# One pass for the clustering and the averaging: frequency products between the clustering's steps

## The chip, the cores and the metric

The kernel runs on one core of a Trainium2 chip. A core has TensorE (matmuls, PE in the rows, with its weight loads as PEld), VectorE (DVE), ScalarE (ACT), GpSimd (POOL), and SyncE (SP), which here issues most DMAs. The metric is the time of one execution on the device in microseconds. All data is float32. TensorE's clock can be granted in full (2.4 GHz, shown as 1.00) or at half (1.2 GHz, shown as 0.50).

## The reference, cut to what matters

Two layers over x of 8 batches x 512 channels x 128 x 128. What matters for the change lies in the first:

```python
x = conv(sx, w_down, stride 2, groups)          # 8 x 256 x 64 x 64, "downsampled"
xx = x[0].reshape(256, 4096); xs = (xx - min) / (max - min)
cent = xs[8 picked rows]                         # k-means over the 256 channels
for _ in range(10):
    d = x2 - 2.0 * (xs @ cent.T) + (cent ** 2).sum(1)
    labels = argmin(d); oh = one_hot(labels); cnt = oh.sum(0)
    cent = where(cnt > 0, oh.T @ xs / max(cnt, 1), cent)
labels = argmin(d of the last cent)
v5 = einsum('bchw,ck->bkhw', x, soh / max(scnt, 1))   # mean map of each cluster, all 8 batches
mu, var = gmm_fit(v5)                            # mixture, 10 steps
gate = sigmoid(...)[labels]; out = bilinear_up_x2(w_up * (gate * x + x)) + sx
```

The second layer projects its input, which is that output, on 64 low cosine frequencies, builds linear attention from these 64 numbers per channel, and adds the result. Since upsampling is linear, the kernel gets those 64 numbers from the frequencies of sx and of the downsampled x. So each batch's downsampled x (256 channels x 4096 positions) is needed for two things in the middle of the kernel: its products with 64 frequency columns (q), and its mean over each cluster's channels.

## The kernel before, in words

The program is five passes, with a barrier between them. Each engine has its own instruction stream, written out by hand; semaphores set the order between the engines, and nothing is reordered by a planner.

1. `first_pass` reads x, makes the downsampled x (`xd`, in HBM) on VectorE, and the frequencies of x (`xps`). A turn on TensorE is four transposes of 128 x 128 (L243) and two products with 64 weight columns and 256 moving ones (L255); ScalarE copies the transposed data from PSUM to SBUF between the two (L217). The two products write the two halves of the PSUM partitions, and two small products (L273) add the halves at a batch's end.
2. `cluster_pass` loads batch 0 of `xd`, normalises it on VectorE (L326 to L331), sums its squares on ScalarE (L384), transposes it (L407, copies L388), and makes the 256 x 256 gram matrix with 64 products (L412), since distances to centroids that are means of rows need only products of rows. Then a loop of 11 rounds with three TensorE steps, each of which waits for VectorE and is waited for: gram times weights (L421, four products, result `dot`), the centroids' squares (L426, two products with ones, `c2`), and the counts (L430, two products with ones). VectorE makes the distances, the labels and the new weights from them in some 15 small instructions. SP also loads here what later passes need (`later`, L316).
3. `average_pass` takes the batches one after another, in two pairs of SBUF buffers that SP fills in turn (L476). A batch is 2 x 4096 columns. 16 groups of four 128-column tiles are transposed (L494), copied by ScalarE (L539) and multiplied with q (L505: the data is the stationary side, 128 weight columns, and q moves, 64 columns). Between the last groups stand eight mean chunks of 512 columns (L516), each two products with 128 weight columns: the labels' weights, placed so that a batch fills its own 16 of 128 rows and zeros the others. VectorE adds each chunk to `ft` (L564).
4. `mixture_pass` reads `ft`, runs the mixture, and ends with the gates (`coef`) and the corrected frequencies.
5. `second_pass` is layer 2 and the output: it streams x in and the result out. It uses the frequency table p in SBUF (`all_p`), which stayed there from the first pass on.

In the change's diff, a wait of SP holds back all that SP issues after it: its DMAs are issued in the order of the code.

## Time and profile before

| | us |
|---|---|
| median of 3 runs (3957.73 to 3962.67) | 3962.45 |
| profiled execution | 3954.77 |
| its span, first to last instruction | 3953.1 |
| first DMA of the clustering pass | 1368.07 |
| first DMA of the averaging pass | 1515.89 |
| first DMA of the mixture pass | 1808.36 |
| first DMA of the second pass | 2127.97 |

Over the span TensorE is busy 83%, VectorE 76%, ScalarE 47%, GpSimd 16%. These shares are means over passes with different limits: from 2300 us on, DMA is busy 96% of the time at 338 GB/s, while between 1409 and 1514 us it is idle. The pages' times count from the first instruction.
### The profile page before, as it was taken

To read this page: it belongs to the slowest core of one execution; us is meant where nothing else is said; L and a number is where in the kernel's file an instruction comes from. 1 tells how busy PE (TensorE), PEld (TensorE's weight loads), DVE (VectorE), ACT (ScalarE), POOL (GpSimd) and SP (SyncE) were. 2 spreads that over 40 slices of the span, in tenths; PEclk is the share of its full clock that TensorE was granted. 3 is DMA by queue.
4 is the path that set the end of the run, shared out by engine and by line. 5 is a ranking of instruction groups with operands and counts; after the bars stand their busy time and mean duration, and the time that the engine had idled before them with its cause. 6 is when DMAs were issued, how large, how long until landed. Compare 5 with 4: busy or idle time off the path is not lost. (4 is left out here: it accounts for less than half of the span.)

```text
span 3953.1 us, 68797 instructions
## 1 busy us (share of the span) xinstructions
PE 3294.6 (83%) x23728; PEld 2450.3 (62%) x23728; DVE 3017.8 (76%) x3492; ACT 1872.6 (47%) x4272; POOL 643.5 (16%) x325
## 2 busy tenths in 40 slices
PE   7999999989999467996665788888989887888877
PEld 3454544545545256774444687777878786877876
DVE  5999999999999732114332697988988797978877
ACT  4555555545555211221112355565665555555654
POOL 0000000000000000000000233333333333333333
PEclk9999999999999767997886899999999999999999
DMA  6556465564655303320002499999999999999998
GB/s 279 238 219 271 197 261 228 230 261 199 267 220 238 132 6 139 127 85 0 0 0 76 150 348 326 347 348 337 347 332 336 326 348 322 350 321 345 353 349 310
DMA packets 348926, 945.53 MB, mean 239 GB/s; under 512 B 25938, under 2 KB 58834, under 8 KB 329491
## 3 DMA queue, kind: packets, MB, share of 16 engines
q1 hardware_dynamic: 339346, 907.41, 62.0%
q0 software_dynamic: 9216, 33.56, 2.1%
q8 instruction: 194, 3.18, 0.3%
q14 instruction: 170, 1.38, 0.1%
HBM read 638.89 MB, written 301.99 MB: 238 GB/s over the span
## 5 line engine op out<-in xcount | busy, mean ns | idle before, releaser
L188 DVE SCALAR_TENSOR_TENSOR first_acc<-first_x,first_wd,first_acc 128x1024 f32<-128x1024 f32 (+1 forms) x1088 | 1297.9, 1273 | 57.7 <-ACT first_acc L213 47.1
L1168 PE MATMUL second_o<-second_right,second_left 128*128 128x128 f32 x8192 | 1107.3, 286 | 187.1 <-POOL second_left L960 123.0
L1168 PEld LDWEIGHTS second_o<-second_right,second_left 128*128 128x128 f32 x8192 | 1024.0, 200 | 240.6 <-issue 217.3
L960 POOL TENSOR_TENSOR second_left<-second_mid_copy,second_coef_rep 64x1024 f32<-64x1024 f32 x256 | 608.7, 2378 | 1974.7 <-ACT second_mid_copy L1274 1967.4
L1413 DVE SCALAR_TENSOR_TENSOR second_x<-second_o,second_shift,second_x 128x512 f32<-128x512 f32 x1024 | 734.4, 738 | 236.9 <-PE second_o L1168 233.4
L217 ACT ACTIVATE first_xT<-first_tp 128x512 f32<-128x512 f32 x1024 | 609.2, 598 | 534.6 <-PE first_tp L243 534.1
L243 PE MATMUL first_tp<-all_const,first_x 128*128 128x128 f32 x4096 | 679.4, 291 | 78.7 <-issue 43.6
L243 PEld LDWEIGHTS first_tp<-all_const,first_x 128*128 128x128 f32 x4096 | 442.2, 144 | 460.6 <-issue 447.5
L255 PE MATMUL first_freq<-first_xT,all_p 128*64 128x256 f32 x4096 | 667.3, 407 | 17.0 <-ACT first_xT L217 7.2
L1253 ACT ACTIVATE second_mid<-second_dd,all_inter 128x128 f32<-128x128 f32 x1024 | 327.1, 390 | 381.1 <-DVE second_mid L1395 370.2
L255 PEld LDWEIGHTS first_freq<-first_xT,all_p 128*64 128x64 f32 x4096 | 210.5, 136 | 192.7 <-issue 178.6
L1253 ACT ACTIVATE second_part<-second_dd,all_inter 128x128 f32<-128x128 f32 x1024 | 323.3, 386 | 0.0
L960 DVE TENSOR_TENSOR second_left<-second_mid_t,second_coef_rep 64x1024 f32<-64x1024 f32 x256 | 309.0, 1207 | 7.1 <-PE second_mid_t L1138 5.3
L1138 PE MATMUL second_mid_t<-all_const,second_mid 128*128 128x128 f32 x1024 | 176.1, 299 | 97.8 <-DVE second_mid L1395 97.8
L163 POOL DMA_DIRECT2D downsampled<-first_acc x64 | 34.3, 536 | 1323.8 <-DVE first_acc L188 1127.9
L1274 ACT ACTIVATE second_mid_copy<-second_mid_t 64x512 f32<-64x512 f32 x256 | 151.6, 592 | 169.0 <-PE second_mid_t L1138 141.6
L564 DVE TENSOR_TENSOR gates_ft<-gates_ft,average_mean 128x512 f32<-128x512 f32 x64 | 44.0, 688 | 239.8 <-PE average_mean L516 239.8
L1138 PEld LDWEIGHTS second_mid_t<-all_const,second_mid 128*128 128x128 f32 x1024 | 129.8, 153 | 115.1 <-DVE second_mid L1395 115.1
L1404 DVE TENSOR_TENSOR second_zt<-all_p,second_rr 128x512 f32<-128x512 f32 x128 | 190.4, 1487 | 0.2 <-DVE second_rr L1388 0.2
L1395 DVE TENSOR_TENSOR second_mid<-second_mid,second_part 128x1024 f32<-128x1024 f32 x128 | 154.7, 1209 | 4.3 <-ACT second_part L1253 4.3
L539 ACT ACTIVATE average_dT<-average_tp 128x512 f32<-128x512 f32 x128 | 74.9, 597 | 168.9 <-PE average_tp L494 168.9
L1277 ACT ACTIVATE second_right<-second_zt_t 64x256 f32<-64x256 f32 x256 | 96.7, 378 | 108.1 <-PE second_zt_t L1151 104.9
(216 smaller groups left out, 2468.2 us busy)
## 6 DMA issues: line engine op xcount, KB each, us to landing
second_x<-in_x SPq DMA_DIRECT2D x512, 512.0 KB, 7.6
out<-second_x SPq DMA_DIRECT2D x512, 512.0 KB, 5.7
first_x<-in_x SPq DMA_DIRECT2D x48, 4224.0 KB, 25.2
first_x<-in_x SPq DMA_DIRECT2D x16, 4096.0 KB
second_dd<-downsampled SPq DMA_DIRECT2D x112, 384.0 KB, 6.5
downsampled<-first_acc POOLq DMA_DIRECT2D x64, 512.0 KB, 11.6
average_xd<-downsampled SPq DMA_DIRECT2D x16, 2048.0 KB, 8.3
second_dd<-downsampled SPq DMA_DIRECT2D x16, 320.0 KB, 6.2
```

The source lines that it names most:

```text
L188: nc.vector.scalar_tensor_tensor(out=acc[c][:, :, left:], in0=tap_window(xt[c], (s, dh, dw), OUT1), scalar=wd[:, t, k:k + 1], in1=acc[c][: ...
L217: nc.scalar.activation(xT[slot][:, :, :], tp[slot][:, :, :], ACT.Copy).then_inc(copied[slot], 1)
L243: last = nc.tensor.transpose(tp[slot][:, n * S + s, :], xt[c][:, s, 1 + r + n, :], ident)
L255: last = nc.tensor.matmul(freq_ps[t][n * UV:(n + 1) * UV, 0:S * P], p_sb[:, row, :], xT[slot][:, n * S:(n + 1) * S, :].rearrange("p s g -> ...
L960: return eng.tensor_tensor(left[a][rows, odd:HALF:2, :, :].rearrange("p n (t s) g -> p n t s g", t=T), turned[rows, :, :, :].unsqueeze(3). ...
L1138: last = nc.tensor.transpose(mid_t[:, n, t, :], mid[m % 2][:, t, r:r + 2, :].rearrange("p h w -> p (h w)"), k("ident"))
L1168: last = nc.tensor.matmul(ob[n][:, r, :], left[a][:, r, n, :], right[a][:, r, :], start=True, stop=True)
L1253: last = nc.scalar.activation((mid[c], part)[r][:, :, 2 * i + 1 - e, :], dd[c][:, :, e + r + i, :], ACT.Copy, scale=row_w[:, 2 * e + r, n ...
L1274: nc.scalar.activation(mid_copy[hi, :, :, :], mid_t[hi, :, :, :], ACT.Copy).then_inc(mid_copied, 1)
L1395: nc.vector.tensor_tensor(mid[c][:, :, :, :], mid[c][:, :, :, :], part[:, :, :, :], ALU.add).then_inc(interpolated, 1)
L1404: nc.vector.tensor_tensor(zt[c][:, :, :], p_sb[:, rows, :], rr[:, rows].unsqueeze(2).broadcast_to([P, ROWS2, UV]), ALU.mult).then_inc(zt_m ...
L1413: nc.vector.scalar_tensor_tensor(out=xt[i][:, n // S, n % S, :, :], in0=ob[n][:, :, :], scalar=shift[:, n:n + 1], in1=xt[i][:, n // S, n % ...
```

## The change

`cluster_pass` and `average_pass` become one `gather_pass`.

- TensorE's stream is a row of 128 units, 16 a batch. A unit is four transposes and the two products of the unit before the last, as in the first pass: q is now the stationary side (64 columns), the data moves (256 columns), two units' halves lie in the two halves of PSUM, and a join of two products adds them at the batch's end.
- Between the units of batches 0 to 4 (80 units) stand the clustering's steps: the transposes of the normalised batch at units 10 to 17 and 22 to 29, the gram matrix in eight blocks at 31 to 38, the eleven rounds at 40 to 72, one step a unit, and the labels at 75.
- Squares are summed in eight pieces on ScalarE. The normalised batch goes to a buffer of its own.
- The means come once the labels are known: for batches 4, 5, 6, 7 at the start of units 80, 96, 112 and 128, from the buffers where these batches lie for their frequencies, and then for batches 0 to 3, which are loaded again. A mean is 16 products with 32 weight columns: four chunks of 512 columns in four column quarters of one PSUM bank, the first and second four chunks in the two 16-row parts of a quarter. VectorE copies the bank, and eight DMAs on SP bring its 16-row pieces to their rows of `ft`. A reload stands behind these eight on SP.
- Four buffers of a whole batch take the SBUF space, so p leaves SBUF after the first pass and is loaded again (4 MB) at the start of the second.

The core of the diff (declarations, and steps that only moved, are cut):

```diff
-def cluster_pass(nc, cst, xd, ohn, oh_t, later):
+RING = 4
+EARLY = 5
+UNITS_F = NT // 2
+MEAN_ORDER = [EARLY - 1, *range(EARLY, B), *range(EARLY - 1)]
+RING_OF_FREQ = [b % 2 for b in range(EARLY)] + [1, 2, 3]
+RING_OF_MEAN = [0, 1, 2, 3, 0, 1, 2, 3]
+XX_AT, GRAM_AT, ITER_AT, LABELS_AT = (10, 22), 31, 40, 75
+def gather_pass(nc, cst, q_cols, xd, ohn, oh_t, ft, xpu, later):
...
             @block.sync
+                load(0, 0)
+                sp.dma_start(q_sb[:, :, :], q_cols.rearrange("p (n k) -> p n k", k=UV)).then_inc(const_in, 16)
+                load(1, 1)
                 for dst, src in later:
                     sp.dma_start(dst, src).then_inc(later_in, 16)
+                for b in range(2, B):
+                    i = RING_OF_FREQ[b]
+                    if i < 2:
+                        sp.wait_ge(transposed, (b - 1) * UNITS_F)
+                        if b == 2:
+                            sp.wait_ge(normal, T)
+                    elif i == 2:
+                        sp.wait_ge(x_turned, T * GROUPS)
+                        sp.wait_ge(squared, T * GROUPS)
+                    else:
+                        sp.wait_ge(gram_made, T)
+                    load(i, b)
+                for n, b in enumerate(MEAN_ORDER):
+                    sp.wait_ge(mean_taken, n + 1)
+                    for r in range(POS // 512):
+                        h, j = r // 4, r % 4
+                        at = 32 * j + 2 * K * h
+                        sp.dma_start(flat[b * 2 * K:(b + 1) * 2 * K, r * 512:(r + 1) * 512],
+                                     rows_sb[n % 2][at:at + 2 * K, :]).then_inc(rows_out[n % 2], 16)
+                    if n < EARLY - 1:
+                        load(RING_OF_MEAN[n + B // 2], MEAN_ORDER[n + B // 2])
...
             @block.vector
+                for n in range(B):
+                    dve.wait_ge(mean_made, n + 1)
+                    if n >= 2:
+                        dve.wait_ge(rows_out[n % 2], n // 2 * (POS // 512) * 16)
+                    nc.vector.tensor_copy(rows_sb[n % 2][:, :], mean_ps[n % 2]).then_inc(mean_taken, 1)
...
             @block.scalar
+                for k in range(ends):
+                    x = x_group(k)
+                    if x:
+                        t, n = x
+                        act.wait_ge(x_turned, t * GROUPS + n + 1)
+                        nc.scalar.activation(xsT[:, 4 * n:4 * n + 4, t, :], bank_x[n % 2][:, :, :], ACT.Copy
+                                             ).then_inc(x_copied, 1)
+                        nc.scalar.activation(square[:, :], xx[t][:, n * 512:(n + 1) * 512], ACT.Square,
+                                             accum_out=x2_parts[:, t, n:n + 1]).then_inc(squared, 1)
...
+                    if k < units:
+                        slot = k % SLOTS
+                        act.wait_ge(transposed, k + 1)
+                        nc.scalar.activation(dT[slot][:, :, :], tp[k % 2][:, :, :], ACT.Copy).then_inc(copied[slot], 1)
...
             @block.tensor
+                pe.wait_ge(const_in, 16)
+                def turn(k):
+                    b, u = k // UNITS_F, k % UNITS_F
+                    i = RING_OF_FREQ[b]
+                    if u == 0:
+                        for t in range(T):
+                            pe.wait_ge(d_in[i][t], loads_before(i, b) * 16)
+                    if k >= 2:
+                        pe.wait_ge(copied[(k - 2) % SLOTS], (k - 2) // SLOTS + 1)
+                    for n in range(2):
+                        for t in range(T):
+                            at = (2 * u + n) * P
+                            last = nc.tensor.transpose(tp[k % 2][:, n, t * P:(t + 1) * P], part(i, t)[:, at:at + P],
+                                                       ident)
+                    last.then_inc(transposed, 1)
...
+                    for n in range(2):
+                        last = nc.tensor.matmul(freq_ps[b % 2][n * UV:(n + 1) * UV, 0:T * P], q_sb[:, 2 * u + n, :],
+                                                dT[slot][:, n, :], start=u == 0, stop=u == UNITS_F - 1)
+                    last.then_inc(multiplied[slot], 1)
...
+                def average(n):
+                    b, i = MEAN_ORDER[n], RING_OF_MEAN[n]
...
+                    if n >= B // 2:
+                        for t in range(T):
+                            pe.wait_ge(d_in[i][t], loads_before(i, B + n - B // 2) * 16)
+                    if n >= 2:
+                        pe.wait_ge(mean_taken, n - 1)
+                    for h in range(2):
+                        for t in range(T):
+                            for j in range(4):
+                                r = 4 * h + j
+                                last = nc.tensor.matmul(mean_ps[n % 2][32 * j:32 * j + 32, :],
+                                                        placed[:, t, (1 - h) * 2 * K:(3 - h) * 2 * K],
+                                                        part(i, t)[:, r * 512:(r + 1) * 512],
+                                                        start=h == 0 and t == 0, stop=h == 1 and t == T - 1)
+                    last.then_inc(mean_made, 1)
+                for k in range(ends):
+                    x = x_group(k)
+                    if x:
+                        turn_x(*x)
+                    if GRAM_AT <= k < GRAM_AT + GROUPS:
+                        make_gram(k - GRAM_AT)
+                    if ITER_AT <= k < ITER_AT + 3 * (ITERS + 1):
+                        iterate(k - ITER_AT)
+                    if k == LABELS_AT:
+                        turn_labels()
+                    if k < units:
+                        turn(k)
+                    if 2 <= k < units + 2:
+                        multiply(k - 2)
+                    b, u = k // UNITS_F - 1, k % UNITS_F
+                    if b >= 0 and u == 5:
+                        join(b)
+                    if k >= EARLY * UNITS_F and k % UNITS_F == 0:
+                        average(k // UNITS_F - EARLY)
+                for n in range(B // 2, B):
+                    average(n)
...
@@ second_pass
                     load_rows(0, 0)
                     load_rows(0, 1)
+                    sp.dma_start(p_sb[:, :, :], p_cols.rearrange("w (h k) -> w h k", k=UV)).then_inc(p_in, 16)
...
                     pe.wait_ge(coef_copied, B)
+                    pe.wait_ge(p_in, 16)
                     for u in range(UNITS):
                         stage(0, u, True)
```

How the instructions of TensorE stand in a round of the clustering before (a product here is one row's count, not two records; `dot`, `c` and `cnt` are the three steps):

```order
302 L407 MATMUL cluster_tp<-all_const,cluster_xx 128x128 x64
303 L412 MATMUL cluster_gram<-cluster_xsT 128x256 x64
304 L417 UNCONDITIONAL_BRANCH
305 L417 ISA
306 L421 MATMUL cluster_dot<-cluster_wt,cluster_gram 128x8 x4
307 L426 MATMUL cluster_c<-cluster_prod,all_const 128x8 x2
308 L430 MATMUL cluster_cnt<-cluster_oh,all_const 128x8 x2
```

And now, from unit 40 on (`gather_x` holds the first two steps' results, `gather_count_ps` the counts):

```order
404 L538 MATMUL gather_x<-gather_wt,gather_gram 128x8 x4
405 L570 MATMUL gather_tp<-all_const,gather_d 128x128 x4
406 L580 MATMUL gather_freq<-gather_dT,gather_q 64x256 x2
407 L544 MATMUL gather_x<-gather_prod,all_const 128x8 x2
408 L570 MATMUL gather_tp<-all_const,gather_d 128x128 x4
409 L580 MATMUL gather_freq<-gather_dT,gather_q 64x256 x2
410 L549 MATMUL gather_count_ps<-gather_oh,all_const 128x8 x2
411 L570 MATMUL gather_tp<-all_const,gather_d 128x128 x4
412 L580 MATMUL gather_freq<-gather_dT,gather_q 64x256 x2
```

A unit of frequency work now stands behind each of the three steps, where TensorE had nothing before.

The means on TensorE before, near the end of each batch:

```order
340 L516 MATMUL average_mean<-average_xd_0,average_placed 128x512
341 L516 MATMUL average_mean<-average_xd_1,average_placed 128x512
342 L494 MATMUL average_tp<-all_const,average_xd_1 128x128 x4
343 L505 MATMUL average_freq<-average_q,average_dT 128x64 x4
344 L516 MATMUL average_mean<-average_xd_0,average_placed 128x512
345 L516 MATMUL average_mean<-average_xd_1,average_placed 128x512
```

And now, at the end of the pass:

```order
621 L580 MATMUL gather_freq<-gather_dT,gather_q 64x256 x4
622 L608 MATMUL gather_count_ps<-gather_d,gather_placed 32x512 x16
623 L580 MATMUL gather_freq<-gather_dT,gather_q 64x256 x2
624 L588 MATMUL gather_freq<-all_const,gather_halves 128x64 x2
625 L608 MATMUL gather_gram_ps<-gather_d,gather_placed 32x512 x16
626 L608 MATMUL gather_count_ps<-gather_d,gather_placed 32x512 x16
627 L608 MATMUL gather_gram_ps<-gather_d,gather_placed 32x512 x16
628 L608 MATMUL gather_count_ps<-gather_d,gather_placed 32x512 x16
```

A batch's mean is one block of 16 products with 32 weight columns (the two PSUM banks that held the gram matrix and the counts take turns), and the last five stand with next to nothing between them.

On SP, the end of the pass now reads:

```order
43 L387 DMA gates_ft<-gather_rows1 16x512 x8
44 L359 DMA gather_d3<-downsampled 128x4096 x2
45 L387 DMA gates_ft<-gather_rows0 16x512 x8
46 L387 DMA gates_ft<-gather_rows1 16x512 x8
47 L387 DMA gates_ft<-gather_rows0 16x512 x8
48 L387 DMA gates_ft<-gather_rows1 16x512 x8
```

The reload of the last batch stands behind eight row DMAs of the mean before it, and the row DMAs of the last four means follow; before, SP issued no row DMAs at all.

## Rows read from the trace of the kernel before

**Rows 1.** Timeline: start us, length us, engine, line, instruction; SP and VectorE.

```profile
1368.07 0.82 SPq L313 DMA_DIRECT2D cluster_xx<-downsampled  x2
...
1371.84 0.36 SPq L316 DMA_DIRECT2D all_gam<-in_gamma  x1
...
1808.36 0.31 SPq L624 DMA_DIRECT2D mix_wc<-in_w_conv  x1
...
1810.67 4.42 DVE L720 TENSOR_REDUCE mix_part<-gates_ft 128x64 f32<-128x4096 f32 x1 [3.15 <-DMA mix_wu<-in_w_up]
```

**Rows 2.** Stages: length, PE, PEld, DVE, ACT, POOL busy (instructions), PEclk, DMA share, GB/s.

```profile
400.00:500.00 100.00, 97.01 (x668) 51.89 (x664) 99.07 (x85) 55.29 (x90) 2.66 (x5) 1.00 0.52 210
...
1368.00:1409.50 41.50, 13.80 (x65) 11.04 (x65) 23.27 (x13) 16.46 (x20) 0.00 (x0) 0.56 0.39 144
...
1443.40:1514.00 70.60, 39.26 (x161) 36.41 (x161) 26.66 (x152) 0.00 (x0) 0.00 (x0) 0.50 0.00 0
...
1562.00:1806.00 244.00, 244.00 (x1570) 187.33 (x1569) 41.10 (x63) 67.32 (x119) 0.00 (x0) 1.00 0.26 103
```

**Rows 3.** Timeline of TensorE in the first two clustering rounds; idle before in brackets.

```profile
1438.02 1.05 PE L421 MATMUL cluster_dot<-cluster_wt,cluster_gram 128*128 128x8 f32 x8 [0.66 <-ACT cluster_gram L392]
...
1439.34 0.61 PE L426 MATMUL cluster_c<-cluster_prod,all_const 128*128 128x8 f32 x4 [0.26 <-DVE cluster_prod L344]
...
1441.32 0.61 PE L430 MATMUL cluster_cnt<-cluster_oh,all_const 128*128 128x8 f32 x4 [1.37 <-DVE cluster_oh L359]
...
1443.38 1.88 PE L421 MATMUL cluster_dot<-cluster_wt,cluster_gram 128*128 128x8 f32 x8 [1.45 <-DVEq L373]
...
1445.52 1.02 PE L426 MATMUL cluster_c<-cluster_prod,all_const 128*128 128x8 f32 x4 [0.26 <-DVE cluster_prod L344]
...
1447.92 1.02 PE L430 MATMUL cluster_cnt<-cluster_oh,all_const 128*128 128x8 f32 x4 [1.37 <-DVE cluster_oh L359]
```

**Rows 4.** Timeline of TensorE in the first pass, at its start and around a batch's end.

```profile
25.47 2.82 PE L243 MATMUL first_tp<-all_const,first_x 128*128 128x128 f32 x12 [25.47 <-DMA all_p<-in_p_cols]
...
28.22 1.02 PE L255 MATMUL first_freq<-first_xT,all_p 128*64 128x256 f32 x4
...
29.17 0.66 PE L243 MATMUL first_tp<-all_const,first_x 128*128 128x128 f32 x4
...
589.55 0.66 PE L243 MATMUL first_tp<-all_const,first_x 128*128 128x128 f32 x4
...
590.72 0.65 PE L243 MATMUL first_tp<-all_const,first_x 128*128 128x128 f32 x4
591.52 1.52 PE L255 MATMUL first_freq<-first_xT,all_p 128*64 128x256 f32 x12
593.51 0.66 PE L273 MATMUL first_sum<-all_const,first_halves 128*128 128x64 f32 x4 [0.47 <-ACT first_halves L220]
```

**Rows 5.** Tile cluster_xx: ns min/median/max, first and last start us; DMA landing.

```profile
L384 ACT ACTIVATE cluster_square<-cluster_xx x2: 3617/3617/3617, 1387.7 to 1399.4; 128x4096 f32<-128x4096 f32 x2
L384 ACT ACTIVATION_READ_ACCUMULATOR cluster_square<-cluster_xx x2: 185/186/187, 1391.3 to 1402.9; 128x1 f32 x2
...
DMA to landing us min/median/max: 12.6/12.6/12.6
```

**Rows 6.** Tile cluster_xsT: the gram products and ScalarE's copies.

```profile
L412 PE MATMUL cluster_gram<-cluster_xsT x128: 379/379/483, 1409.5 to 1437.0; 128*128 128x256 f32 x128
L388 ACT ACTIVATE cluster_xsT<-cluster_tp x16: 576/597/599, 1391.3 to 1408.8; 128x512 f32<-128x512 f32 x16
```

**Rows 7.** Timeline of the averaging pass: one mean chunk and what follows it.

```profile
1540.66 1.94 PE L516 MATMUL average_mean<-average_xd,average_placed 128*128 128x512 f32 x4
...
1542.43 0.60 PE L494 MATMUL average_tp<-all_const,average_xd 128*128 128x128 f32 x4
```

**Rows 8.** Stages: ten us near the start of the second pass.

```profile
2136.00:2146.00 10.00, 7.67 (x32) 6.87 (x32) 1.28 (x3) 1.79 (x3) 0.00 (x0) 0.50 1.03 376
```

**Rows 9.** Timeline of the second pass: TensorE's first product that follows the new wait.

```profile
2158.93 5.31 PE L1049 MATMUL second_st<-all_wv,second_xp 128*64 128x512 f32 x8 [6.98 <-DVE second_xp L1354]
```

346 lines of the change are left out of this document (152 added, 194 removed).

## Prediction, written before the changed kernel ran

> **What bounds it now.** I read the views in this order: the whole span by stages with the granted clock, then the stretch between the two passes over x in order of time, then single tiles for what one instruction takes.
>
> The change lies between the first DMA of the clustering pass, at 1368.07 us, and the first DMA of the mixture pass, at 1808.36 us [rows 1]: 440.3 us. All eight batches are averaged after the clustering. In the stages [rows 2] TensorE is busy 39.3 of 70.6 us in the iterations, at clock 0.50, the lower level (1.2 GHz), and 244.0 of 244.0 us at 1.00 (2.4 GHz) in averaging. So the first half of this stretch is bound by a chain of small steps between TensorE and VectorE at a low clock, and the second by TensorE alone.
>
> An iteration took 5.36 us at the high clock (1438.02 to 1443.38) [rows 3]. The later ones go at the lower one: there the four gram products take 1.88 us instead of 1.05, and the two ones-products 1.02 instead of 0.61.
>
> All this is of the profiled execution: span 3953.1, time 3954.8 us. The median of the three runs is 3962.45, 7.7 us above it; I add that at the end.
>
> **The unit of the new loop.** 128 units of four transposes and two frequency products (now 64 weight columns, 256 moving ones) are what the first pass does per turn, with the same shapes. There a turn starts at 589.55 and the next at 590.72: 1.17 us at the high clock [rows 4]. At the low clock twelve transposes took 28.22 - 25.47 = 2.75 us and the two products 29.17 - 28.22 = 0.95, so a unit is 4 x 0.229 + 0.95 = 1.87 us. The low clock lasted 3.7 us after TensorE's start there.
>
> **The sum up to unit 80** (us from 1368.07):
> - Start. TensorE first waits for q, queued behind batch 0. Both halves of batch 0 had landed 12.6 us after issue [rows 5]; q is a quarter of their bytes, so about 2.6 more: 15.2.
> - Units 0 to 9: some 4 us at the low clock are two units, the other eight 9.4: 13.6. The first normalised half was ready at 1387.7, the second at 1399.4 (the squares start there [rows 5]); units 10 and 22 come later than that, so no wait for VectorE.
> - Units 10 to 17 and 22 to 29 also turn a group of the normalised batch. TensorE would need 1.17 + 4 x 0.12 = 1.65. ScalarE does two copies of 512 columns at 0.60 [rows 6], a square of 512 (an eighth of 3.62 would be 0.45; I take a copy's 0.60) and an accumulator read of 0.19 [rows 5]: 1.99, and it is what ends last. 16 x 1.99 = 31.8. Bounds 1.65 and 2.2 each (waits between): 26 to 35.
> - Five plain units (18 to 21, 30): 5.9.
> - Gram, eight blocks of eight products. 128 records start over 27.5 us, 0.217 each [rows 6]; eight products are 16 records, 3.5, and a unit 1.17: 8 x 4.66 = 37.3. Unit 39: 1.2. TensorE does this work as before, and nothing hides it.
> - Iterations, 11 x 3 units. The gram products take 1.05, then a unit 1.17: 2.22, more than the 1.32 that VectorE needs until the next step. From the c2 products to the counts took 1.98 and from the counts to the next gram products 2.06 [rows 3]; there 0.61 + 1.17 = 1.78 fit in. So 2.22 + 1.98 + 2.06 = 6.26, and 68.9 for eleven. This is the heart of the gain: the 33 units (38.6 us) cost almost nothing, and TensorE idles 0.5 of 6.26 us.
> - Units 73 to 79 and two turned labels: 8.7. Four joins (a batch's two halves added, four records, 0.66 as in the first pass's fold [rows 4]): 2.6.
>
> Together 15.2 + 13.6 + 31.8 + 5.9 + 37.3 + 1.2 + 68.9 + 8.7 + 2.6 = 185.2.
>
> **From unit 80 on.** 48 units and three joins: 56.2 + 2.0, to 243.4. To this the means. Before, a chunk's two products (four records of 512 columns) took 1542.43 - 1540.66 = 1.77 us [rows 7], eight chunks 14.2 a batch. Now there are again 16 products a batch, as many columns each, but with 32 weight columns in one quarter of the array. No row shows quarters. Bounds: one after another, 14.2; four at a time, 3.5. The nearest row is the run of twelve records on two halves: 1.52 us from first start to last end [rows 4], where one at a time needs 12 x 0.217 = 2.6. Halves gave the full two, so I take the full four: 3.5.
>
> The Trainium skill ("TensorE: Matmul & The Clock Gate", Part 3: Packing small matmuls) says that matmuls start strictly in program order. Since a product is two records on one quarter, neighbours alone could overlap then, two at a time: 7.1 a batch, a rival below. The trace speaks against it: in strict order the twelfth record would start six steps of 0.217 after the first and end 0.38 later (a record's drawn length [rows 6]), 1.68 and not 1.52. By the same part's 2.38 times for three column tiles, a batch would be an estimated 4.5 us, and the sum some 6 us higher.
>
> Means 0 to 3 stand in the loop: 4 x 3.5, to 257.4. After that, the last batch's products and join take 1.9 and means 4 to 6 10.5, but mean 7 needs batch 3 loaded again into the buffer that mean 3 frees: VectorE's copy 0.9 (ScalarE's takes 0.60, and a wake-up), eight row DMAs queued on SP ahead of the load at 0.54 each (seven issues from 1368.07 to 1371.84 [rows 1]) 4.3, landing 12.6, together 17.8. That is later than 12.4, so the load decides: 275.2, mean 7 to 278.7. Then the tail that the old pass had not: copy 0.9, eight issues 4.3, landing 2.3 (as 1808.36 to 1810.67 [rows 1]), end of the pass 0.8: 287.0. The other reloads have 18 us or more of units to hide in. The 64 additions of VectorE go away, but they lay beside a TensorE that was busy all the time.
>
> **Outside the stretch.** The first pass is unchanged. The second pass loads p again, 4.2 MB, behind the first rows of downsampled data and ahead of x. DMA moved 376 GB/s between 2136 and 2146 [rows 8], so p is 11.2 us of it, and lands before 2150. TensorE and VectorE wait for it ahead of work that began at 2158.93 [rows 9]. x comes 11 us later than it did, before any sum needs it. I cost it at 0; if the cover went, 11.2.
>
> **Total.** 440.3 - 287.0 = 153.3 saved. 3954.8 - 153.3 = 3801.5, plus 7.7: **3809 us**.
>
> **Rivals.**
> 1. *Quarters only in pairs.* 7.1 a batch: 243.4 + 28.4 + 1.9 + 21.3 + 7.1 + 8.3 = 310.4, the reload now hidden. Saved 129.9: 3833. For it: nothing in the trace runs more than two at once. Against: the full overlap of halves.
> 2. *Quarters don't run in parallel at all,* so that this part of the change doesn't do what it says: 243.4 + 56.8 + 1.9 + 56.8 + 8.3 = 367.2, saved 73.1: 3889. Against: halves do.
> 3. *The iterations stay at the low clock.* A low-clock iteration needs 1.88 + 1.87, and twice 1.02 + 1.87: 9.5 us instead of 6.26. 11 x 3.3 = 36: 3845. For it: clock 0.50 through the old iterations with TensorE busy 56% of the time. Against: it is now busy 92%, with units that held 1.00 in the first pass [rows 2].
> 4. *Slower: the low clock holds in the whole new pass.* Units 128 x 1.87 = 239.4, turned groups 14.7, gram 55.8, iterations' own products 11 x 3.92 = 43.1, joins 9.1 + 2.9, means in pairs at half speed 113.6, labels 0.6, start and tail 23.5: 502.7, 62.4 more than now: 4025. With four quarters at once it is 445.9, or 3968. It becomes slower once more than 129.9 / 192.3 = 68% of the pass is at the low clock. For it: the clock is 0.50 when the pass starts, and 0.56 on average until the gram products [rows 2]. Against: the old averaging pass, a mix of the same kinds, held 1.00 for 244 us.
>
> On rival 4, the skill (same page, Part 4: PE-mode transpose) says that transposes do not hold the high clock as matmuls do, and here transposes are half of a unit. By that rule alone rival 4 would be likely. The trace does not agree: the first pass, made of the same units, has 1.00 over 100 us [rows 2].
>
> **Chances.** Forecast 57%, pairs 25%, not parallel 5%, iterations at the low clock 8%, whole pass low 2%, other 3%. The forecast's terms move by -9 (group turns at 1.65, smaller tail) and +15 (waits in the iterations, slower landing), so 3800 to 3824. The range takes in pairs and most of the low iterations: 3790 to 3855. It leaves out about a fifth. A measurement of this kernel tells 0.2%, 8 us, from no change: faster 97% (all but rival 4 and a part of "other"), within 1%, slower 2%.
>
> **What would show it.** Units 1.17 us apart at clock 1.00; iterations 6.3 us apart; a mean's 16 products in 3.5 us (7.1 for pairs); a gap of about 5 us ahead of the last mean, filled by the reload; first mixture DMA 287 us after the first load; second pass as long as now. Wrong would be: a clock of 0.50 past unit 10, ScalarE late in plain units, or TensorE held by a reload of batches 0 to 2.

## The result, and the profile of the changed kernel

The changed kernel takes 3865.89 us (median of 4 runs, 3862.28 to 3875.95), the kernel before 3960.09 in the same comparison. The ratio is 0.976, 95% interval 0.973 to 0.980. The forecast was 3809 us, with a range from 3790 to 3855: the sign was right, the size not. 94 us were gained where 153 had been worked out. Between the two profiled executions, 3954.8 and 3866.2 us, the gain is 88.6, 65 less than worked out.

The profiled execution has a span of 3864.6 us. It shows where the 65 us are (the first loads are issued at 1368.07 and 1368.89 us):

| stretch | before | forecast | measured |
|---|---|---|---|
| first load to first mixture DMA | 440.3 | 287.0 | 318.1 |
| of that, first load to the first mean | | 185.2 | 209.3 |
| of that, first mean to the end | | 101.8 | 108.8 |
| first mixture DMA to the labels' last products | 311.2 | unchanged | 344.4 |
| from there to the end | 1833.5 | unchanged | 1833.2 |

The fourth row of the table ends at these products, in the kernel before and in the changed one (ns min/median/max, first and last start us):

```profile
L688 PE MATMUL mix_l<-mix_ymat,gates_oh_t x4: 361/361/380, 2119.6 to 2120.3; 128*128 128x8 f32 x4
```

```profile
L757 PE MATMUL mix_l<-mix_ymat,gates_oh_t x4: 361/362/383, 2031.4 to 2032.0; 128*128 128x8 f32 x4
```

So the forecast failed in two places: 31 us in the new pass, and 33 us in the mixture pass, whose code was not touched.

Stages of the changed kernel, to be held against [rows 2]. Columns: stretch, length, busy time of PE, PEld, DVE, ACT and POOL, granted clock, DMA share, GB/s.

```profile
1368.90:1467.50 98.60, 83.24 (x512) 57.82 (x512) 23.64 (x15) 40.95 (x92) 0.00 (x0) 0.90 0.51 200
1467.50:1480.00 12.50, 11.15 (x85) 7.51 (x83) 5.26 (x30) 3.91 (x8) 0.00 (x0) 1.00 0.00 1
1481.00:1569.70 88.70, 88.70 (x367) 58.58 (x366) 24.08 (x139) 17.60 (x32) 0.00 (x0) 0.50 0.46 190
1569.70:1655.00 85.30, 84.66 (x626) 40.81 (x628) 2.96 (x5) 34.69 (x64) 0.00 (x0) 1.00 0.43 160
1655.00:1721.00 66.00, 23.48 (x136) 10.84 (x128) 29.11 (x51) 6.39 (x11) 0.00 (x0) 0.63 0.27 81
1721.00:2038.00 317.00, 219.66 (x934) 134.25 (x934) 92.64 (x252) 42.41 (x68) 0.00 (x0) 0.72 0.00 0
```

Row 1 is the way to the clustering rounds, row 2 the first two rounds, row 3 most of the others. There TensorE is busy for the whole 88.7 us, and yet at 0.50. A busy share of 100% does not say that the clock is up. Row 4 is the units with the means, row 5 the end of the pass, row 6 the mixture's rounds.

TensorE in the first round, and in a later one, by the timeline (start us, us, engine, line, instruction, and in brackets the idle time before):

```profile
1467.54 1.06 PE L538 MATMUL gather_x<-gather_wt,gather_gram 128*128 128x8 f32 x8
...
1469.60 0.61 PE L544 MATMUL gather_x<-gather_prod,all_const 128*128 128x8 f32 x4
...
1471.58 0.61 PE L549 MATMUL gather_count_ps<-gather_oh,all_const 128*128 128x8 f32 x4 [0.30 <-DVE gather_oh L436]
...
1473.65 1.06 PE L538 MATMUL gather_x<-gather_wt,gather_gram 128*128 128x8 f32 x8 [0.38 <-DVEq L450]
```

```profile
1495.27 1.02 PE L549 MATMUL gather_count_ps<-gather_oh,all_const 128*128 128x8 f32 x4
1496.14 1.09 PE L570 MATMUL gather_tp<-all_const,gather_d 128*128 128x128 f32 x4
1497.17 1.12 PE L580 MATMUL gather_freq<-gather_dT,gather_q 128*64 128x256 f32 x4
1498.22 1.88 PE L538 MATMUL gather_x<-gather_wt,gather_gram 128*128 128x8 f32 x8
```

The first round takes 1473.65 - 1467.54 = 6.11 us, with 0.68 us of waiting in it, where 6.26 was forecast. At the low clock a unit takes 1498.22 - 1496.14 = 2.08, and a round is 3 x 2.08 + 1.73 + 2 x 0.87 = 9.7 us. Nothing waits there: at 0.50 TensorE has more work than the round's chain through VectorE has room for.

A mean, and the end of the pass:

```profile
1578.23 3.64 PE L608 MATMUL gather_gram_ps<-gather_d,gather_placed 128*32 128x512 f32 x32
...
1655.50 1.06 SPq L359 DMA_DIRECT2D gather_d<-downsampled  x2
1656.60 27.83 SPq L387 DMA_DIRECT2D gates_ft<-gather_rows  x32
...
1671.45 5.57 PE L608 MATMUL gather_count_ps<-gather_d,gather_placed 128*32 128x512 f32 x32 [9.85 <-issue]
1673.71 0.69 DVE L461 COPY gather_rows<-gather_gram_ps 128x512 f32<-128x512 f32 x1 [14.78 <-DMA gates_ft<-gather_rows]
...
1686.98 0.30 SPq L693 DMA_DIRECT2D mix_wc<-in_w_conv  x1
```

The mean of a batch is 32 records in 3.64 us. A chunk of [rows 7], four such records one at a time, took 1.77, so eight chunks took 14.2: four quarters run at once, as forecast. At the end 32 row DMAs leave SyncE in 27.83 us, 0.63 us apart, with a wait of 7.6 us for VectorE's copy after the first sixteen. TensorE idles 9.85 us ahead of the last mean, and VectorE's copy of the mean before it stands 14.78 us behind rows that have not left their buffer.

A round of the mixture, before and after. Columns as above:

```profile
2005.30:2032.60 27.30, 18.46 (x93) 11.91 (x93) 8.48 (x24) 4.38 (x7) 0.00 (x0) 0.87 0.00 0
```

```profile
1964.75:1995.48 30.73, 21.87 (x93) 13.32 (x93) 8.49 (x23) 4.38 (x7) 0.00 (x0) 0.72 0.00 0
```

TensorE has the same 93 records, and VectorE and ScalarE are busy as long as before (8.48 and 8.49 us, 4.38 and 4.38). What differs is the clock, 0.72 on average for 0.87, and with it TensorE's busy time. Ten rounds of 3.4 us more are the 33 us.

### The profile page after: what moved, and what is told of

Its sections match the earlier page's. It is cut to its first block and busy times, and to the rows that moved or that the text cites. A ratio compares the mean times of both kernels' runs of the same rounds, so it can differ in the third digit from the quotient of the medians.

```text
span 3864.6 us, 67478 instructions
## 1 busy us (share of the span) xinstructions
PE 3242.6 (84%) x23248; PEld 2339.7 (61%) x23248; DVE 2977.1 (77%) x3431; ACT 1874.3 (48%) x4307; POOL 646.0 (17%) x325
## 5 line engine op out<-in xcount | busy, mean ns | idle before, releaser
L1240 PE MATMUL second_o<-second_right,second_left 128*128 128x128 f32 x8192 | 1106.6, 286 | 186.4 <-POOL second_left L1031 110.7
L256 PE MATMUL first_freq<-first_xT,first_p 128*64 128x256 f32 x4096 | 669.6, 408 | 17.1 <-ACT first_xT L218 7.5
L256 PEld LDWEIGHTS first_freq<-first_xT,first_p 128*64 128x64 f32 x4096 | 211.0, 136 | 192.9 <-issue 177.9
L1477 DVE TENSOR_TENSOR second_zt<-second_p,second_rr 128x512 f32<-128x512 f32 x128 | 193.6, 1512 | 0.2 <-DVE second_rr L1461 0.2
L488 ACT ACTIVATE gather_dT<-gather_tp 128x512 f32<-128x512 f32 x128 | 76.3, 598 | 216.2 <-PE gather_tp L570 216.0
L747 PE MATMUL mix_c<-gates_feat,mix_resp 128*16 128x128 f32 x640 | 99.0, 334 | 57.9 <-DVEq L875 57.9
```

The lines of the kernel that those rows point to most:

```text
L256: last = nc.tensor.matmul(freq_ps[t][n * UV:(n + 1) * UV, 0:S * P], p_sb[:, row, :], xT[slot][:, n * S:(n + 1) * S, :].rearrange("p s g -> ...
L1240: last = nc.tensor.matmul(ob[n][:, r, :], left[a][:, r, n, :], right[a][:, r, :], start=True, stop=True)
L1477: nc.vector.tensor_tensor(zt[c][:, :, :], p_sb[:, rows, :], rr[:, rows].unsqueeze(2).broadcast_to([P, ROWS2, UV]), ALU.mult).then_inc(zt_m ...
```

## Experiments: why the clock fell in the clustering rounds

Theory A: the rounds' own products move 8 columns behind a full load of weights. They fill TensorE's time with little work, and for that the clock falls. I first added one wide product a round whose result is never read.

```
+                    if ITER_AT <= k < ITER_AT + 3 * (ITERS + 1) and (k - ITER_AT) % 3 in (2,):
+                        for _ in range(1):
+                            nc.tensor.matmul(mean_ps[0], ident, cst[:, 0:512], start=True, stop=True)
```

> The changed kernel with one more product of 512 columns on TensorE per clustering round (11 in all, behind the unit that follows the count products; its result is never read). In the changed kernel the third and later rounds go at granted clock 0.50 and take 9.58 to 10.57 us, the first two 6.11. A 512-column product is two records of 0.44 us at the high clock, 0.89 us, and at the low clock 1.77. Theory A (the clock falls because the rounds' own products have only 8 moving columns behind a full weight load, so that TensorE is busy by the records but does little): the filler brings the work per round up and the rounds keep 1.00; TensorE idles about 0.5 of 6.1 us, so a round is 6.1 + 0.4 = 6.5, and the nine late rounds save about 3.3 each, 30 us in all: first mixture DMA about 290 us after the first load instead of 318, time near 3836. If one filler is not enough the clock stays low and each round gets 1.8 us longer, 11.6 us, time near 3883. Rival B (the clock falls for a reason that has nothing to do with what TensorE does there, such as the time since the kernel began or what the other engines do): the rounds stay at 0.50 whatever is added, 11.6 us each, 3883.

Measured: all eleven rounds at 1.00, 6.51 to 6.60 us each but the last with 6.96. The pass took 289.7 us. The median is 3804.14 us (3797.85 to 3835.53, 5 runs), the ratio to before 0.961 (0.956 to 0.966); the traced run is the one at 3835.53.

```profile
1469.00:1541.00 72.00, 69.02 (x469) 44.65 (x469) 29.46 (x169) 20.84 (x39) 0.00 (x0) 1.00 0.45 181
```

More work on the engine that bounds the stage made the stage a third shorter. Theory A stands, and a fall that does not depend on TensorE is out. With three fillers a round the question was whether more helps more:

> The changed kernel with one more product of 512 columns on TensorE behind the unit of every clustering step (33 in all, results never read). Theory A (too little work in the rounds' 8-column products): with three fillers a round the high clock holds; a round is TensorE-bound at 6.1 - 0.5 + 3 x 0.89 = 8.3 us, against 9.7 to 10.6 now, so nine late rounds save 1.4 each and the first two cost 2.2 each: about 8 us less than the changed kernel, 3857. Rival B (the clock falls whatever TensorE does): 9.7 + 3 x 1.77 = 15 us a round, 55 us more, 3920.

Measured: rounds of 7.87 us at 1.00 (two of 8.31), the pass 306.2 us, median 3846.64 (3825.81 to 3856.58; the traced run, the lowest, has short mixture rounds, on which more below). One filler is enough, and the others cost their own time. The expected 8.3 us a round was a little too much.

The rival that remained: it is the idle 0.68 us of a round that counts, and any product that fills it would do. So about the same TensorE time with four products of 8 moving columns (`K` is 8) instead of one of 512:

```
-                        for _ in range(1):
-                            nc.tensor.matmul(mean_ps[0], ident, cst[:, 0:512], start=True, stop=True)
+                        for _ in range(4):
+                            nc.tensor.matmul(mean_ps[0][:, 0:K], ones, cst[:, 0:K], start=True, stop=True)
```

> The changed kernel with four more products of 8 columns per clustering round, in the place where the run before had one product of 512 columns (44 in all, results never read). Four such products are eight records; eight records of the same shape take 0.95 us at the high clock, as long as the 512-column product does (0.89), so TensorE is kept busy as long and its idle time shrinks as much, but with 32 columns of moving data instead of 512. With the 512-column product all eleven rounds stayed at 1.00 and took 6.5 us. Theory A1 (the work in the records counts, and 8-column products are next to none): the clock falls after two rounds as in the changed kernel, late rounds take 9.7 + 1.9 = 11.6 us, the pass 336 us instead of 318, time near 3884. Rival A2 (TensorE's idle time of 0.5 us per round counts, and any product that fills it will do): rounds of 6.55 us at 1.00, pass 290 us, time near 3804 to 3836.

Measured: the clock falls even earlier, after one round, and stays at 0.50 for 119.5 us. Late rounds take 11.42 us and two 12.27; the pass takes 341.5 us. The traced run took 3886.14, the median is 3865.48 (3852.6 to 3886.14).

```profile
1468.00:1475.00 7.00, 6.70 (x54) 4.98 (x53) 2.63 (x15) 1.96 (x4) 0.00 (x0) 1.00 0.01 2
1475.20:1594.70 119.50, 119.50 (x504) 84.70 (x503) 26.83 (x154) 20.48 (x38) 0.00 (x0) 0.50 0.34 141
```

Ahead of the fall TensorE was busy 6.70 of 7.00 us, 96%, exactly as with the wide filler between the same two times (6.70 of 7.00; 69.02 of the 72.00 above). With equal busy time one keeps 1.00 and the other does not, and rival A2 is out. The two fillers differ in what they move, 512 columns or 32, and in how many records and weight loads they are, two or eight. If it is what they move, useful work should do as well as a filler. A unit is eight records too, but four of them are transposes and four move 256 columns each. Four units a round (the gram blocks stand closer, so that the rounds begin at unit 35):

```
-XX_AT, GRAM_AT, ITER_AT, LABELS_AT = (10, 22), 31, 40, 75
+XX_AT, GRAM_AT, ITER_AT, LABELS_AT = (10, 22), 31, 35, 79
+GRAM_UNITS = 4
...
+                    if GRAM_AT <= k < GRAM_AT + GRAM_UNITS:
+                        make_gram(2 * (k - GRAM_AT))
+                        make_gram(2 * (k - GRAM_AT) + 1)
+                    if ITER_AT <= k < ITER_AT + 4 * (ITERS + 1) and (k - ITER_AT) % 4 < 3:
+                        iterate((k - ITER_AT) // 4 * 3 + (k - ITER_AT) % 4)
```

> The changed kernel with four units of frequency work per clustering round where it has three, and no filler: the gram products stand two blocks to a unit, so that the rounds begin at unit 35, and end at 79, ahead of the first mean as now. A unit has, in its two products, 512 columns of moving data like the filler, and its four transposes. Theory A1 (the clock stays up if TensorE has enough real work per round): all rounds at 1.00 and 6.1 - 0.5 + 1.17 = 6.8 us, 74.8 for eleven instead of 104 now, and eleven units of 1.17 less outside the rounds, 12.9: the pass takes 318 - 29 - 13 = 276 us, time 3866 - 42 = 3824 with mixture rounds of 30.7, 3791 with 27.3. Rival A3 (the filler held the clock because it is dense without a break, and transposes with small products don't do the same): the clock falls after two rounds, late ones take 9.7 + 1.87 = 11.6 us: 318 + 14 - 13 = 319, time 3867 or 3834.

Measured: 6.83 us a round (three of 7.27), all at 1.00, and 44 units of frequency work stand in the rounds where 33 did. The pass took 281.3 us where 276 was expected, the median is 3827.99 (3803.94 to 3833.41).

```profile
1463.00:1537.00 74.00, 70.73 (x524) 46.59 (x524) 28.55 (x165) 26.66 (x50) 0.00 (x0) 1.00 0.49 197
```

Rival A3 falls: eight more records a round hold the clock when they are a unit, and do not when they are 8-column products. By the Trainium skill ("TensorE: Matmul & The Clock Gate", Part 4: PE-mode transpose) transposes do not hold the high clock as matmuls do. Here sixteen of them a round, with the units' products, held it; what did not was the 8-column products. So for this loop it is shown that a TensorE kept busy with 8-column products falls to 0.50 where one kept as busy with wider ones does not; how wide they have to be was not measured.

## Experiments: why untouched mixture rounds got longer

The mixture's rounds have a gap of 5.79 us in which TensorE waits for VectorE's responsibilities. Theory C: the clock falls in such gaps, and the length of a round depends on where the low stretches meet TensorE's work.

```
+                    for _ in range(6):
+                        nc.tensor.matmul(tp[1][:, :, :].rearrange("p j k -> p (j k)"), k("ident"),
+                                         feat[:, 0:4, :].rearrange("p n k -> p (n k)"), start=True, stop=True)
                     pe.wait_ge(resps, i + 1)
```

> The changed kernel with six products of 512 columns on TensorE in the gap of each mixture round, ahead of the wait for the responsibilities (results never read). In that gap TensorE idles 5.79 us of a round of 30.72; six fillers are 5.3 us at the high clock. In the changed kernel a mixture round has 17 us at granted clock 0.50 in two stretches, in the kernel before 6.8 us of 27.3. Theory C (the clock falls in the mixture's rounds because TensorE idles there, and how much of a round is low depends on where the falls meet the work): with the gap filled the rounds stay at 1.00 for most of their length; by the kernel before (27.3 us with 6.8 low, which cost 3.4) a round all at the high clock is about 24 us, so 10 x 6.8 = 68 us saved, time near 3798. If the gap ahead of the parameters (2.0 us) still lets it fall, one low stretch of 6.8 stays: 27.3 a round, 3832. Rival D (the longer rounds come from the place of the tiles in SBUF or from the data's way in, not from the clock): rounds stay at 30.7 or get longer by what the fillers overhang, 3866 or more.

Measured: rounds of 26.9 us at clock 0.94, two of 25.2 at 1.00; median 3824.94 us (3824.54 to 3831.07).

```profile
1825.20:1852.10 26.90, 23.20 (x106) 13.60 (x105) 8.51 (x23) 4.38 (x7) 0.00 (x0) 0.94 0.00 0
1773.10:1798.30 25.20, 21.50 (x106) 13.01 (x105) 8.50 (x23) 4.38 (x7) 0.00 (x0) 1.00 0.00 0
```

So the clock sets the length of a round, and rival D is out. I had expected 24 us a round and 3798: a round all at 1.00 needs 25.2, and a short low stretch stayed in most. But why 30.7 us in the changed kernel and 27.3 before? Among the variants above, whose mixture code is the same, the traces of rounds_fill3 and same_quarter (below) had 27.3, those of rounds_fill1 and rounds_narrow 30.7. I moved the start of the loop a little:

```
+                for _ in range(2):
+                    ch.link(nc.vector.memset(wide[:, :], 0.0))
                 ch.link(nc.vector.memset(moment_rows[:, :], 0.0))
```

> The changed kernel with two more memsets of 1.0 us on VectorE just ahead of the mixture's loop: the loop starts 2.2 us later, and nothing else changes. In the changed kernel a mixture round takes 30.7 us in every run so far; the same code took 27.3 in the kernel before and in two of four variants of the changed kernel. Theory C1 (where the loop's first round falls against the steps of the clock sets which of two repeating patterns the rounds fall into): the rounds can come out at 27.3, and the time at 3866 + 2 - 33 = 3835. Rival C2 (something else of the changed kernel makes them 30.7, such as what ran before or where its tiles lie): 30.7, time 3868.

Measured: two runs at 3829.47 and 3836.47, two at 3866.71 and 3866.73. In the trace, of the run at 3836.47, rounds take 27.31:

```profile
1776.17 0.17 DVE L704 COPY mix_mu<-mix_a 128x16 f32<-128x16 f32 x1 [0.77 <-PE mix_b L700]
...
1803.48 0.17 DVE L704 COPY mix_mu<-mix_a 128x16 f32<-128x16 f32 x1 [0.77 <-PE mix_b L700]
...
1830.79 0.17 DVE L704 COPY mix_mu<-mix_a 128x16 f32<-128x16 f32 x1 [0.77 <-PE mix_b L700]
```

The one program has two times some 33 us apart. Then the changed kernel itself might have both:

> The changed kernel as it is, run more often. Its four executions so far took 3862 to 3876 us, and its trace has mixture rounds of 30.72 us. The kernel before ran mostly near 3955 and four times in fourteen at 3984 to 4005; the version with two more memsets, otherwise this kernel, ran twice at 3829 to 3836 (trace: rounds of 27.31) and twice at 3867. Theory C1 (which of two patterns the mixture's rounds fall into differs from execution to execution of the same program): of six more executions some take about 33 us less, 3833, and the rest 3866. Rival C2 (the pattern belongs to the program, and the extra memsets changed it): all six at 3862 to 3876.

Measured: 3863.55 to 3869.74 five times, and once 3834.76. So of ten executions of the changed kernel one is 31 us under the others. Of 29 of the kernel before, in all comparisons, 21 took 3948 to 3965 us and 8 took 3985 to 4005. Traces show 27.3 us a round in the lower group (the kernel before, the version with two memsets) and 30.7 in the upper (the changed kernel, twice); no program was traced in both. That the runs without a trace differ for the same reason is inferred, from the equal distance and from their mean clock: 0.928 at 3834.76 and 0.914 to 0.917 at the other five; 0.926 to 0.930 in the lower group of the kernel before, 0.913 to 0.919 in the upper. The step fits: a long round has 17.0 us at 0.50 and a short one 6.8, so ten long rounds lower the mean over 3866 us by an estimated 0.013.

Rival C2 falls in its strong form: by the times, neither pattern belongs to a program. But their shares differ, 8 of 29 long before the change and 9 of 10 after it. What sets the share is open. That it depends on where the loop's start falls in time fits the version with two memsets, two of four long, but four runs are too few to show it.

## Experiments: the means and the end of the pass

Do neighbours in the order of products have to lie on different quarters?

```
-                    for h in range(2):
-                        for t in range(T):
-                            for j in range(4):
+                    for j in range(4):
+                        for h in range(2):
+                            for t in range(T):
```

> The changed kernel with the sixteen products of each batch's mean in another order: all four of one column quarter, then the four of the next, where now neighbours go to different quarters. Same products, same result. Now a mean takes 3.57 to 3.64 us. Theory E (products start strictly in program order and overlap only because neighbours lie on different quarters): only the last product of one quarter and the first of the next overlap, 16 x 0.885 less three overlaps of 0.885 is 11.5 us a mean, 8 us more each. In the loop all of this is on TensorE's path: eight means, 63 us, less what the reload's wait before the last mean hides: near 3920. Rival F (each quarter takes its products from a queue of its own, and order between quarters does not matter): 3.6 us a mean, no change, 3866.

Measured: 8.86 us a mean, so both theories are wrong. The pass took 340.9 us; the median is 3854.3 only because the traced run, and perhaps others, had the short mixture rounds.

```profile
1578.38 8.86 PE L608 MATMUL gather_gram_ps<-gather_d,gather_placed 128*32 128x512 f32 x32
```

Single records say more. In the changed kernel the 32 records start in eight groups of four, 6 to 7 ns apart within a group and 0.43 us from group to group. In this version four start alone, 0.43 us apart; 6 ns behind the fifth starts a sixth, which the trace does not name but which can only be the next quarter's first, since two records of one quarter start 0.43 us apart. Twelve of the 32 start 6 to 30 ns behind another, which makes 20 steps x 0.43 = 8.6 us. So records of a later quarter do start ahead of earlier ones, but only a few places ahead: eight records of one quarter in a row are too many. What sets how far ahead was not tested. The Trainium skill ("TensorE: Matmul & The Clock Gate", Part 3: Packing small matmuls) says that matmuls start strictly in program order. Neither trace agrees: here the program's ninth record starts ahead of its sixth, and in the changed kernel, where a product is two records on one quarter, groups of four could not be.

The tail. First, the reload ahead of the rows (and no longer behind them):

```
+                    if n < EARLY - 1:
+                        sp.wait_ge(mean_made, n + 1)
+                        load(RING_OF_MEAN[n + B // 2], MEAN_ORDER[n + B // 2])
                     sp.wait_ge(mean_taken, n + 1)
...
-                    if n < EARLY - 1:
-                        load(RING_OF_MEAN[n + B // 2], MEAN_ORDER[n + B // 2])
```

> The changed kernel with the order of SyncE's work behind each of the first four means turned round: the reload of a batch is issued when TensorE has made the mean, ahead of VectorE's copy and the eight row DMAs, where now it comes behind them. Theory (the last mean waits for the reload, which waits for 0.69 us of copy and 5.1 us of row issues): the last mean starts 5.8 us earlier, and the pass takes 312 us instead of 318. Rival (the tail is set by the 32 row DMAs of the last four means, 0.63 us each on SyncE, which the reload's place does not shorten by more than its own two issues): 317. In time 3860 or 3865, if the mixture's rounds stay at 30.7; the pass is read from the trace.

Measured: the pass takes 317.6 us for 318.1. The rival is right.

```profile
1649.20 0.81 SPq L359 DMA_DIRECT2D gather_d<-downsampled  x2
...
1668.13 0.69 DVE L461 COPY gather_rows<-gather_count_ps 128x512 f32<-128x512 f32 x1 [12.78 <-DMA gates_ft<-gather_rows]
1668.97 5.04 PE L608 MATMUL gather_count_ps<-gather_d,gather_placed 128*32 128x512 f32 x32 [7.51 <-DVE gather_rows L461]
```

The last mean now waits for a copy that waits for a row buffer, where it had waited for the reload; the reload 6.3 us earlier bought 2.5 us at the last mean, and 0.5 at the end. Why the buffer was so late stands in the landings, which the expectation left out. In the changed kernel the first sixteen rows issued behind the reload of 4 MB landed 8.2 to 12.8 us after their issue, the last sixteen 1.9 to 2.0:

```profile
L387 SPq DMA_DIRECT2D gates_ft<-gather_rows x16: 512/589/719, 1656.6 to 1666.3; - x16
...
DMA to landing us min/median/max: 8.2/11.3/12.8
```

```profile
L387 SPq DMA_DIRECT2D gates_ft<-gather_rows x16: 507/589/592, 1674.4 to 1683.8; - x16
...
DMA to landing us min/median/max: 1.9/2.0/2.0
```

With the reload moved, sixteen rows still stood behind it, and landed 8.1 to 13.5 us after their issue. So two things hold the end up, the issues and rows that land late beside a reload. (The median of this version, 3833.2 with runs from 3829 to 3874, says nothing of this edit: one of its five runs has the long mixture rounds, four by their times the short ones.) Next, four row buffers in memory that is free by then, and the last four means' rows from SyncE and ScalarE in turn:

```
-                    for r in range(POS // 512):
-                        h, j = r // 4, r % 4
...
+                    rows_of(sp, n, range(POS // 512) if n < B // 2 else range(0, POS // 512, 2))
...
+                for n in range(B // 2, B):
+                    act.wait_ge(mean_taken, n + 1)
+                    rows_of(act, n, range(1, POS // 512, 2))
```

> The changed kernel with the reload ahead of the rows, four buffers for the rows instead of two, and the 32 row DMAs of the last four means issued by SyncE and ScalarE in turn, 16 each. With the reload moved alone the pass stayed at 318 us: the copy of mean 5 waited 12.8 us for a free row buffer and held up the last mean, and 40 row DMAs went out one after another over 33.8 us. Theory (the tail is the row DMAs: buffers and 0.63 us an issue): now the last mean waits for the reload alone (issued at 1649, landing 12.6 to 16 us later), 5.6 us, a copy, four issues at 0.63 and a landing of 2.3: pass 308 us, 10 less. Rival (the landing of rows and reload in the shared DMA engines is what takes the time, whoever issues them): 316 or more.

Measured: the pass 310.7 us, median 3825.46 (3824.39 to 3855.36). That is 7.4 us less of the 10 expected. Against the version before it, the last mean starts 1.6 us earlier and the stretch behind it is 5.2 us shorter; buffers and second queue were not tried apart. With both engines issuing at once, four issues took 2.42 us on the one and 2.74 on the other, where eight take one engine 8 x 0.63 = 5.0. Two queues almost halve the time:

```profile
1654.46 2.42 SPq L361 DMA_DIRECT2D gates_ft<-gather_rows  x4
```

```profile
1654.46 2.74 ACTq L361 DMA_DIRECT2D gates_ft<-gather_rows  x4
```

The last mean now waits for the reload alone, and a part of the rival is true:

```profile
1666.33 5.91 PE L617 MATMUL gather_count_ps<-gather_d,gather_placed 128*32 128x512 f32 x32 [5.79 <-issue]
```

The reload's second half landed at 1666.23, 17.6 us after its issue, where 12.6 to 16 had been allowed for. So at least 1.6 of the 2.7 us that are missing are landing and not issue.

## Experiments: faster versions

First rounds_fill1, mix_fill6 and reload_first in one kernel, and a second filler in the mixture:

```
+                    for _ in range(2):
+                        nc.tensor.matmul(tp[1][:, :, :].rearrange("p j k -> p (j k)"), k("ident"),
+                                         feat[:, 0:4, :].rearrange("p n k -> p (n k)"), start=True, stop=True)
                     pe.wait_ge(weights, i + 1)
...
```

> All that helped together, as a version to beat both: one 512-column product per clustering round, six such products ahead of the wait for the responsibilities in each mixture round and two more ahead of the wait for the weights (a gap of 2.0 us), and the reload ahead of the rows. The pass: 290 us (measured with the filler) less 6 for the reload is 284. The mixture: a round with no low clock in it took 25.2 us when the first gap was filled, and most took 26.9 with 3.4 us low; if the second filler keeps the clock up all ten take 25.2, so 344.4 - 10 x 5.5 = 289 us. Time 3866 - 34 - 55 = 3777. If the second filler does not help: ten rounds of 26.7, 3792. If it is late at the weights and costs its own overhang: 3800.

Measured: 3773.88 us (3767.53 to 3782.10), ratio 0.949 (0.941 to 0.956), and 3777 was expected. The pass takes 290.2 us and the mixture's rounds 25.2 at 1.00; its four runs lie within 15 us, with no group of long ones:

```profile
1768.30:1793.50 25.20, 23.31 (x110) 13.62 (x109) 8.50 (x24) 4.38 (x7) 0.00 (x0) 1.00 0.00 0
```

Then units4 in the place of the clustering filler, and rows_two_queues in the place of reload_first; the mixture's two fillers stay:

```
-XX_AT, GRAM_AT, ITER_AT, LABELS_AT = (10, 22), 31, 40, 75
+XX_AT, GRAM_AT, ITER_AT, LABELS_AT = (10, 22), 31, 35, 79
...
```

> The fast version once more, with useful work where its clustering rounds had a filler: four units a round, rows on two queues out of four buffers, the reload ahead of the rows, and in the mixture's rounds six and two fillers of 512 columns as before. The version with fillers ran at 3773.9 us. If units hold the clock as the filler did, and the tail gets 10 us shorter: the pass takes 276 - 10 = 266 us instead of 290, 3750. If the clock falls in the rounds: pass 309, 3793. The mixture's rounds are expected at 25.2 us.

Measured: 3772.0 us (3765.27 to 3782.95), ratio 0.951 (0.946 to 0.957). The traced pass takes 273.4 us, 16.7 less than in the version before, and the traced run is 17 us shorter than that version's. But the runs without a trace, 3771 to 3783 against 3767 to 3774, are no shorter. What took the 17 us back in them is open. The two versions are the same by this measurement, and both beat the changed kernel by some 2.4% (by 1.6% its one execution with short mixture rounds, 3834.76).

## Why the forecast was wrong, step by step

- *Up to the rounds:* right. Units 1.17 us apart at 1.00. The first gram product of round one stood 98.6 us behind the first load, where the terms add up to 106.3 (with the two joins that lie there): the group turns took 1.61 us each, by the lower bound of 1.65 and not the 1.99 of ScalarE's work in a row.
- *The rounds, 11 x 6.26:* this step failed. Rival 3, which I gave 8%, is what happened. Two rounds took 6.11 us, then the clock fell. I had held against that rival that TensorE was "now busy 92%, with units that held 1.00 in the first pass". The trace and rounds_narrow show why that does not follow: busy time is no measure of the work. The 8-column products take 1.85 us of a round of 6.11 (0.91, 0.47 and 0.47 from start to next start), and do little. The rival's own price was near: 9.5 us a round for 9.7 measured, and 3845 in all. The time came out 21 us above it for another reason, the mixture pass; in an execution with short mixture rounds it was 3834.8. From round one to the first mean it took 110.7 us where the terms gave 78.9: 31.8 more, less the 7.7 saved ahead. (1.2 of it is a unit that the sum forgot, since the first mean stands behind unit 80.)
- *Means, 3.5 us each with four quarters at once:* right, 3.57 to 3.64 (5.57 for the last one, at the low clock). Rivals 1 and 2 are out. I had argued from halves to quarters; same_quarter shows that the order of products carries it.
- *The tail, 17.8 for the reload and 8.3 behind the last mean:* the reload did decide when the last mean starts, but 22.2 us behind mean 3. It landed 15.9 us after its first issue, where 12.6 was taken from [rows 5], and the eight issues ahead of it took 5.4 for 4.3. Behind it the last mean, most of it at the low clock, took 2 us more, and rows of the mean before it still stood in the queue. I had not seen that rows issued behind a reload land with it, and so hold two row buffers and VectorE's copy. Together 7 us.
- *Second pass:* right. The reload of p cost nothing, 1833.2 us for 1833.5.
- *The mixture pass at no change:* 33 us wrong. That its rounds have two lengths could not be seen in one trace, but [rows 2] show the clock falling in stages with gaps, and the mixture's own clock of 0.87 a round was there to be asked about. Three timed runs of before, all of the short kind, did not show it either. Against executions of the same kind the change is worth 3957.7 - 3834.8 = 123 us in the short one and 3993.1 - 3866.2 = 127 in the long one (medians of the groups): the 153 forecast less 31 for the pass. So it is luck on which side of the range's upper end, 3855, the median fell: the one short execution in ten, 3834.8, lies inside, with the step of the rounds as wrong as before.
- *Rival 4, slower:* did not come near. About 20 us at the start (0.90 over 98.6 us), 88.7 in the rounds and some 15 at the end were at the low clock, 39% of the pass, where 68% was the point of no gain.

## What to carry to other kernels

Where TensorE shares a stage with a chain of tiny products, read the granted clock beside the busy share, and price the stage at both levels: one 512-column product of no use per round took 28 us off a pass here, and one unit of useful work more per round took 37. A loop whose rounds have gaps on TensorE may have more than one stable length; before you give a few tens of us to an edit, look at the lengths of such loops in both traces and at single executions, and fill the gap if you want them to be one. Products that are to run at once on different column quarters belong next to each other in the program. Small DMAs that free a buffer belong ahead of a large load in a queue, or the buffer has to be spare: here they landed after 2 us by themselves and after 8 to 13 behind the load.

## What the runs showed of the hardware

- The clock fell to 0.50 while TensorE was busy 96% of the time, with four 8-column products added to each round, and stayed there through 119.5 us at 100%; with one 512-column product a round in their place, at 96% too, it stayed at 1.00.
- An unchanged loop ran at 27.3 us a round in one kernel's trace and at 30.7 in another's; by their times and mean clocks, executions of one program differ in the same way.
- Four quarters of fp32 products of 512 columns ran at once, 32 records in 3.64 us. With eight records of a quarter in a row, another's record started 6 ns behind the fifth (which quarter's, by the program's order), and the mean took 8.86 us.
- A small DMA from SBUF to SBUF took 0.63 us of SyncE's time to issue, and landed 2.0 us after its issue, or 8.2 to 12.8 when it was issued behind a load of 4 MB.
